# A two-convolution kernel: a later filter and even portions, loads in long rows, and two operations moved from VectorE to ScalarE

## The reference

```
x = x + wavelet_conv(groupnorm(x), w0, w1, w2, bias)
x = x + local_filter(groupnorm(x), spatial_weight)
```

```
dot        = einsum('bchw,bckhw->bkhw', x, patches)
sim        = dot / max(norm_x * norm_p, 1e-8)
weight     = (sim + 1) / 2 * spatial_weight[k]
out        = einsum('bckhw,bkhw->bchw', patches, weight)
```

## Time and profile before

| | |
|---|---|
| median of 3 runs | 2198.71 us |
| the profiled execution's own time | 2198.1 us |
| its span, first to last instruction | 2196.5 us |
| TensorE busy, matmuls | 76% of the span |
| VectorE busy | 69% |
| ScalarE busy | 29% |
| mean granted TensorE clock | 0.825 of full |
| HBM traffic | 238.7 MB read, 86.6 MB written |

### The profile page before, as it was taken

One profiled execution on the slowest core, in us unless ns is written; L12 is line 12 of the kernel. 1 busy time (PEld: TensorE's weight loads), 2 busy tenths in 40 slices (PEclk: granted clock), 3 DMA queues, 4 the chain that ended last, 5 costly groups with the idle time before them and its releaser, 6 DMA issues.

```text
span 2196.5 us, 49122 instructions
## 1 busy us (share of the span) xinstructions
PE 1666.1 (76%) x16895; PEld 883.3 (40%) x16895; DVE 1506.4 (69%) x2313; ACT 629.4 (29%) x1030; POOL 448.3 (20%) x791
## 2 busy tenths in 40 slices
PE   4777796787877797778877786778878787775575
PEld 3543353334433353334433353334433343332343
DVE  6427767876588567876588667885678666785564
ACT  2321232223332232323333232323223132322331
POOL 1352331014200232013300242012400242011000
PEclk8978997879878897788878897788978898777555
DMA  5252366564955567663956466564955567563775
GB/s 167 77 126 77 113 166 164 153 157 115 223 139 152 149 168 162 154 169 108 222 135 154 129 171 169 138 179 114 222 131 159 137 159 180 126 177 103 167 170 126
DMA packets 216642, 329.95 MB, mean 150 GB/s; under 512 B 51189, under 2 KB 182261, under 8 KB 215797
## 3 DMA queue, kind: packets, MB, share of 16 engines
q1 hardware_dynamic: 174832, 207.19, 38.4%
q0 software_dynamic: 41472, 118.24, 19.7%
HBM read 238.70 MB, written 86.61 MB: 148 GB/s over the span
## 4 chain that ended last, share of the span: by engine, by line
DVE 29%; PE 25%; issue 17%; SPq 13%; DMA 12%; DVEq 2%; ACT 2%; POOL 0%; POOLq 0%; ACTq 0%
PE conv L1258 7%; DMA unit_mem<-d_n 6%; DMA d_n<-st_n 5%; SPq L390 5%; DVE wgt L980 4%; PE conv L1232 4%; PE gram L1320 4%; SPq L398 4%; PE out_ps L1342 2%; PE vals_ps L1303 2%; DVE eo L795 2%; PE conv L1217 2%; DVE st_n L928 2%; DVE st_a L926 2%; PE conv L1441 2%
## 5 line engine op out<-in xcount | busy, mean ns | idle before, releaser
L1258 PE MATMUL conv<-thl,wconv 128*128 128x496 f16 (+2 forms) x1920 | 574.6, 431 | 20.8 <-DVE xa L855 8.3
L980 DVE SCALAR_TENSOR_TENSOR wgt<-gram,tapw 124x512 f32<-124x512 f32 x512 | 347.9, 688 | 349.2 <-PE gram L1320 316.5
L454 POOL DMA_DIRECT2D ring<-in_x x576 | 333.7, 584 | 322.3 <-ACT xa L538 222.4
L1320 PE MATMUL gram<-unit_mem 128*60 128x128 f16 x4096 | 267.6, 259 | 119.6 <-DVE wgt L980 114.7
L1342 PE MATMUL out_ps<-wgt,vals 124*32 124x128 f32 x4096 | 199.8, 323 | 122.5 <-DVE wgt L980 98.1
L1320 PEld LDWEIGHTS gram<-unit_mem 128*60 128x60 f16 x4096 | 164.3, 121 | 315.1 <-issue 309.0
L1258 PEld LDWEIGHTS conv<-thl,wconv 128*128 128x128 f16 x1920 | 174.2, 107 | 254.1 <-issue 120.5
L1232 PE MATMUL conv<-thl,wconv 128*128 128x480 f16 (+7 forms) x1200 | 251.7, 367 | 0.0
L538 ACT ACTIVATE vals<-vals_ps 124x512 f32<-124x512 f32 x128 | 76.2, 595 | 419.5 <-PE vals_ps L1303 419.5
L1342 PEld LDWEIGHTS out_ps<-wgt,vals 124*32 124x32 f32 x4096 | 115.2, 124 | 188.3 <-DVE wgt L980 124.1
L488 POOL DMA_DIRECT2D up<-d_z x128 | 68.6, 539 | 596.9 <-DVE xa L909 566.5
(11 more groups left out here) (132 smaller groups left out, 2007.2 us busy)
## 6 DMA issues: line engine op xcount, KB each, us to landing
unit_mem<-d_hl SPq DMA_DIRECT2D x512, 180.0 KB
ring<-in_x POOLq DMA_DIRECT2D x288, 128.0 KB, 3.4
ring<-in_x POOLq DMA_DIRECT2D x288, 127.0 KB, 3.5
d_hl<-st_hl SPq DMA_DIRECT2D x64, 360.0 KB
d_v<-st_v SPq DMA_DIRECT2D x64, 360.0 KB
unit_mem<-d_v SPq DMA_DIRECT2D x128, 180.0 KB
up<-d_z POOLq DMA_DIRECT2D x160, 128.0 KB, 2.8
d_x<-x POOLq DMA_DIRECT2D x32, 512.0 KB, 4.2
```

The costliest lines, as they stand in the source:

```text
L454: pool.dma_start(dst, src).then_inc(raw_in[slot], 16)
L980: V.scalar_tensor_tensor(out=dst, in0=g, scalar=SIM_SCALE ** 2, in1=tapw[:, :].unsqueeze(1).to_broadcast([KN, 2, 2 * QN]), op0=ALU.add, op ...
L1258: last = mm(dst[:, :, b0:b1], wconv0[:, w, 2 * (p % ROWS4) + s, dx + 2, :], thl[:, p % 2, d, s, :, b0 + dx:b1 + dx] if p % ROWS4 != 1 else ...
L1320: last = mm(bank[row:row + KQ, col:col + QN], key[:, q, e_at, TH * KW * g:TH * KW * g + KQ], tile[:, :, TH * g + 1:TH * g + 1 + TH, 1:1 + ...
```

## The change

It has four parts.

1. **TensorE's order.** The last `filter_group` of a unit moves into the next unit (portion 1); `key_values` of the unit moves from before its first gram product to behind its second, and its second half from portion 4 to 5. The first three `filter_group` move from portions 3, 5, 7 to 4, 5, 7. The `norm_piece` of unit `j + 2` move from portions 1, 2 to 0, 2. PE's wait for the unit's load stands where it stood, before the first gram product. SyncE's wait before loading over the buffer of unit `u - 2` is now for its gram products and turned values, not for its last `filter_group`.
2. **VectorE's portions.** The two to four instructions of `accumulate`, `finals`, `wino_in` and `image_stats`, which ran in one portion, are spread over two to four portions. `value_lows` moves from portion 2 to 0, `result` from 1 to 2, `wino_low` from 2 to 1. Four of the eight `raw_stats` of the next image go from the opening into unit 0, and the other four to the end of the opening; the first group norm's small operations go from units 0 and 1 to units 1 and 2.
3. **Long-row loads.** In DRAM a half is now laid out as [part, channel, quadrant, 720] instead of [partition, part, 720]. A load of keys, queries or values reads rows of 4 x 720 f16 (5760 B) where it read rows of 720 (1440 B), and there are 7 such loads instead of 10. The saves are 5 instead of 3; a save of a part writes from 128 partitions to a DRAM pattern whose leading dimension is the quadrant, with 4 entries.
4. **ScalarE.** The square of the root (line 920) becomes a ScalarE `Square`. The count of small norms (line 935) becomes a ScalarE `Sign` of 1.0001 - norm with a sum, and `set_flag` turns the sum of signs to a count. The second piece of `vals_out` moves behind `keep_point`.

The diff, cut to its core:

```
@@ sync: save_half, load_unit
-                sp.dma_start(d_hl[b, h], st_hl[:, :, h % 2, :]).then_inc(half_saved, 16)
-                sp.dma_start(d_v[b, h], st_v[:, :, h % 2, :]).then_inc(half_saved, 16)
+                for hl in range(2):
+                    sp.dma_start(d_hl[b, h, hl].rearrange("c q n -> q c n"), st_hl[:, hl, h % 2, :]).then_inc(half_saved, 16)
+                for hl in range(2):
+                    sp.dma_start(d_v[b, h, hl].rearrange("c q n -> q c n"), st_v[:, hl, h % 2, :]).then_inc(half_saved, 16)
...
                 if u >= 2:
-                    sp.wait_ge(group_done, START + 4 * (8 * b + u - 1))
+                    sp.wait_ge(gram_ready, 8 * (8 * b + u - 1))
+                    alone(sp)
+                    sp.wait_ge(vt_ready, 16 * b + 2 * (u - 1))
...
-                for dst, order in ((keys[s], (0, 1, 0, 1)), (queries[s], (0, 0, 1, 1))):
-                    for j, hl in enumerate(order):
-                        sp.dma_start(dst[C * j:C * j + C].rearrange("c q e n -> c q (e n)"),
-                                     d_hl[b, u, :, hl, :].rearrange("(q c) n -> c q n", c=C)).then_inc(unit_in[s], 16)
-                for hl in range(2):
-                    sp.dma_start(values[s][C * hl:C * hl + C].rearrange("c q e n -> c q (e n)"),
-                                 d_v[b, u, :, hl, :].rearrange("(q c) n -> c q n", c=C)).then_inc(unit_in[s], 16)
+                for j in range(2):
+                    sp.dma_start(keys[s][2 * C * j:2 * C * (j + 1)].rearrange("c q e n -> c (q e n)"),
+                                 d_hl[b, u].rearrange("l c q n -> (l c) (q n)")).then_inc(unit_in[s], 16)
+                for j, hl in enumerate((0, 0, 1, 1)):
+                    sp.dma_start(queries[s][C * j:C * j + C].rearrange("c q e n -> c (q e n)"),
+                                 d_hl[b, u, hl].rearrange("c q n -> c (q n)")).then_inc(unit_in[s], 16)
+                sp.dma_start(values[s][0:2 * C].rearrange("c q e n -> c (q e n)"),
+                             d_v[b, u].rearrange("l c q n -> (l c) (q n)")).then_inc(unit_in[s], 16)
@@ scalar
+                if p == 1:
+                    act.wait_ge(n2_kept, START + 16 * b + 2 * h + 2)
+                    act.wait_ge(unit_low, START + 8 * b + h)
+                    copy(st_b[:, :], st_a[:, :], func=ACT.Square).then_inc(root_squared, 1)
+            def count_own(b, h):
+                act.wait_ge(prep_link, 8 * PREP_LINKS * b + PREP_LINKS * (h + 1))
+                act.wait_ge(unit_low, START + 8 * b + h)
+                nc.scalar.activation(st_hl[:, 1, h % 2, 0:UN], st_n[:, h % 2, :], ACT.Sign, bias=edge[:, :], scale=-1.0,
+                                     accum_out=short[:, h % 2:h % 2 + 1]).then_inc(short_kept, 1)
...
                 for j in range(CONV_TILES):
-                        vals_out(b, j, 0)
...
                     if conv and j + 1 < CONV_TILES:
                         wino_high(i, j + 1)
                     if ls and j + 2 < 2 * BANDS:
-                        norms(b, j + 2)
+                        norms(b, j + 2, 0)
                     if ls:
-                        vals_out(b, j, 1)
+                        vals_out(b, j, 0)
+                    if ls and j + 2 < 2 * BANDS:
+                        norms(b, j + 2, 1)
                     if conv:
                         keep_point(i, j)
                     if ls:
+                        vals_out(b, j, 1)
                         if j + 2 < 2 * BANDS:
+                            count_own(b, j + 2)
                             unit_highs(b, j + 2)
@@ vector
-                ch.link(dve, V.tensor_tensor(st_b[:, :], st_a[:, :], st_a[:, :], ALU.mult))
+                dve.wait_ge(root_squared, 8 * b + h + 1)
...
-                prep_chain.link(dve, V.tensor_scalar(st_b[:, :], st_n[:, h % 2, :], 1.0001, None, ALU.is_lt, ALU.add,
-                                                     accum_out=short[:, h % 2:h % 2 + 1]))
...
                 if conv:
-                    for c in range(SLOTS):
-                        raw_stats(i + 1, c)
                     wino_delta(i, 0)
...
+                    raw_stats(i + 1, 0)
+                    raw_stats(i + 1, 1)
                     level1_out(i, 0)
...
                     level1_out(i, 1)
-                    raw_stats(i + 1, SLOTS + 2)
-                    raw_stats(i + 1, SLOTS + 3)
+                    raw_stats(i + 1, 2)
+                    raw_stats(i + 1, 3)
...
-                            if k == 1 and j > 0:
+                            if k == 2 and j > 0:
                                 result(b, j - 1)
-                            if k == 1 and j in (1, 3, 5, 7):
-                                accumulate(i, j - 1)
+                            if k in (1, 2) and j in (1, 3, 5, 7):
+                                accumulate(i, j - 1, k - 1)
+                            if k == 1 and j + 1 < CONV_TILES:
+                                wino_low(i, j + 1)
+                            if k < 4 and j == 0:
+                                raw_stats(i + 1, SLOTS + k)
-                            if k == 5 and j + 2 < CONV_TILES:
-                                wino_in(i, j + 2)
+                            if k in (6, 7) and j + 2 < CONV_TILES:
+                                wino_in(i, j + 2, k - 6)
@@ tensor: the hook of portion k in unit j
-                                key_values(b, j, 0)
+                                unit_here(b, j)
                             if k == 4:
-                                key_values(b, j, 1)
+                                filter_group(b, j, 0)
                             if k < PAIRS:
                                 gram(b, j, k, short_ones[0])
-                            if k in (3, 5, 7, 8):
-                                filter_group(b, j, (k - 3) // 2 if k < 8 else 3)
+                            if k == 1:
+                                if j > 0:
+                                    filter_group(b, j - 1, 3)
+                                key_values(b, j, 0)
+                            if k == 5:
+                                filter_group(b, j, 1)
+                                key_values(b, j, 1)
+                            if k == 7:
+                                filter_group(b, j, 2)
```

More of the change, by code:

```diff
@@ L639, in vals_out @@
                 act.wait_ge(vt_ready, 16 * b + 2 * u + part + 1)
-                act.wait_ge(group_done, START + 4 * (8 * b + u))
+                act.wait_ge(group_done, START + 4 * (8 * b + u) - (2 if u > 0 and part == 0 else 0))
                 copy(vals[:, 16 * part:16 * part + 16, :].rearrange("p n c -> p (n c)"), vals_ps[0:KN, :]).then_inc(vals_done, 1)
@@ L676, in iteration @@
                 for j in range(CONV_TILES):
-                    if ls:
-                        vals_out(b, j, 0)
-                    if conv and j == 1:
+                    if conv and j == 2:
                         root(gn1, gn1_var, gn1_root, i + 1)
@@ new lines, in wino_in @@
+                if step != 1:
+                    dve.wait_ge(t_ready, 8 * i + p)
+                    if kind == 0:
+                        wino_chain.link(dve, V.tensor_tensor(e2, two_rows(delta, 3), two_rows(delta, 1), ALU.subtract))
+                        wino_chain.link(dve, stt(e2, two_rows(xa, H0 // 2 * half + 3), -2.25, e2))
+                    elif kind == 1:
+                        wino_chain.link(dve, V.tensor_tensor(t2, two_rows(delta, 4), two_rows(delta, 0), ALU.add))
+                    elif kind == 2:
+                        wino_chain.link(dve, stt(e2, two_rows(delta, 3), 4.0, two_rows(delta, 1), op1=ALU.subtract))
+                    else:
+                        wino_chain.link(dve, stt(e2, two_rows(delta, 1), -4.0, two_rows(delta, 3)))
@@ new lines, in wino_in @@
+                if step != 0:
+                    if kind == 0:
+                        V.tensor_tensor(point[0], even, odd, ALU.add)
+                        V.tensor_tensor(point[1], even, odd, ALU.subtract).then_inc(t_wide, 1)
+                    elif kind == 1:
+                        stt(t2, two_rows(delta, 2), -4.25, t2).then_inc(t_wide, 1)
+                    else:
+                        far = 2.0 if kind == 2 else 0.5
+                        stt(point[0], odd, far, even)
+                        stt(point[1], odd, -far, even).then_inc(t_wide, 1)
@@ L878, in accumulate, with finals @@
                     dve.wait_ge(live_kept, n + 1)
[L879 to L886 removed]
+                acc = two_rows(xa, 2 + H0 // 2 * half + 2 * pair)
+                if kind == 0:
+                    stt(acc, acc, x_gain, s2).then_inc(acc_step, 1)
+                else:
+                    stt(acc, s2, 1.0 if pair == 0 else 4.0, acc).then_inc(acc_step, 1)
+            def finals(n, half, pair):
                 dve.wait_ge(acc_step, acc_count(n, 4 * half, SUMS_AT[3]))
@@ L1013, in iteration @@
                     sums(b, 7)
-                    finals(b, 1)
```

(5 more changed lines are left out.)

135 lines of the change are left out of this document (58 added, 77 removed).

## The result

The changed kernel takes 2318.35 us (median of 4 runs, 2315.27 to 2328.09) against 2197.97 of the kernel before beside it: 1.055 times, 95% interval 1.052 to 1.059. It is 5.5% slower where I had forecast 2067 us and a gain of 6%. The profiled execution took 2328.09 us for a span of 2326.5.

What follows compares the result with a forecast made beforehand. It took an exchange between VectorE and TensorE, read per stage, as the bound. From 2198.1 us, -144 for seven iterations and +13 for iteration 8 gave 2067, chance 0.52, own range 2030 to 2105; 8 in 10: 1978 to 2165.

Steps and rivals of the forecast that it cites:

- The bound of before, parts 1 and 2: Units 1 to 5: VectorE and TensorE wait on each other; VectorE's idle time falls from 4.2 to 1.5 us per unit.
- Part 4: Units 1 to 5: VectorE loses 1.64 us per unit, 8.2 us in all; ScalarE's added 1.4 us per unit is hidden.
- Rival C: Norms-to-split chain: table loads or late values copy make a unit some 23 us, about 2124 us; 0.20 with milder rival B.
- Part 3, the saves: Four large saves run on four DMA engines, 7.8 us in place of 2.0; loads begin after 10.1 us, not 4.2.
- the collision: Unit 0: four later raw rows collide with unit 1's load; unit 0 taken as 23.0 us, between 21 and 27.
- Both are under 20.8, but only just.: SyncE's 19.6 us and the save-and-load round trip's 20.1 per unit stay under VectorE's 20.8 us.
- SyncE's cycle: Per unit: save 10.1, load 7.0, store and residual every two units; 19.6 us with gaps, against 15 before.
- rival B: Save packets take 96 ns, a save 12.3 us; every unit waits for SyncE's cycle of 24.1 us; 2247 us, chance 0.13.
- The signs: Loads begin 10 us after first save if right, 6 Rival A, 14 rival B; units 1 to 5 over 115: core wrong.
- The sum: -18.2 + 1.4 - 2.2 - 1.6 = -20.6 us per iteration, -144 for seven; iteration 8 +13; 2067 us.
- The long rows: Loads: rows of 5760 B can't be slower per byte; seven issues replace ten, 7.0 us in place of 8.4.
- Rival A: Saves get 16 engines, SyncE's cycle is 15 us, VectorE alone binds, 104 us for units 1 to 5; 1972 us, chance 0.15.

## Why the prediction was wrong

**The bound of before, parts 1 and 2: right.** The pause at the change of unit is gone, and where no load is late VectorE is idle 1.9 and 2.2 us per unit (units 1 and 4 of the change, mean of seven), 1.5 forecast.

**Part 4: right.** VectorE's work in units 1 to 5 is 96.7 us, as forecast. ScalarE's square takes 713 ns (0.715 taken), the sign 804 plus 187 to read its sum (0.7 taken, 0.3 too little, which shows in no stretch). Rival C is refuted: still two table loads, and the variant with the new ScalarE work is the faster one.

```profile
L548 ACT ACTIVATE st_b<-st_a 128x612 f32<-128x612 f32 x64 | 45.6, 713 | 2.0
L548 ACT ACT_TABLE_LOAD x2 | 2.6, 1283 | 15.1 <-PE conv L1479 11.8 <-DVE gn L792 3.3
L651 ACT ACTIVATE st_hl<-st_n,edge 128x612 f16<-128x612 f32 x64 | 51.5, 804 | 61.0 <-DVE st_n L957 60.7
L651 ACT ACTIVATION_READ_ACCUMULATOR st_hl<-st_n,edge 128x1 f32 x64 | 12.0, 187 | 0.0
```

**Part 3, the saves: this step failed, by its size.** Four engines was right. "128 packets of 61 ns, 7.8 us in place of 2.0, so the loads begin after 10.1 us" was not. Three things were missing.

- The pace alone is 66 ns, which is 0.6 us over 128 packets, and the loads begin after 11.1 to 13.0 us even in the quiet units.
- I took that quiet time for all eight saves of an iteration. Three of them run beside raw rows and upsampled data and take 14.8 to 22.3 us. The forecast named the collision, "four raw rows now come later and collide with this load", and gave unit 0 23.0 us; it took 34.2. Beside q0 the save gets 1.4 engines of its four, and when q0 is through it still has only four, while twelve stand idle. The row for the crowd was there: 98% busy in the earlier trace rows.
- A load's landing took 4.7 us in quiet, against 2.9 taken from the earlier trace rows. The 13.7 beside raw rows is no part of the miss, since the kernel before had it too and unit 0 was forecast as a difference from it.

**The comparison that decided: "Both are under 20.8, but only just."** SyncE's cycle was put at 19.6 us. In iteration 8 it is 22.3 over a pair of units: 19.6 (2176.50 to 2196.07) in a unit without store and residual, 25.0 in one with them. The forecast's terms make 17.1 of the first (10.1 + 7.0). It lacks 1.7 us of save (2176.50 to 2188.30 is 11.8), 0.5 of load (2188.30 to 2195.83 is 7.5) and the gap; store and residual add 5.4 where 4.0 were taken. With that the bound passes from VectorE to SyncE, as rival B had it. B's mechanism and side are right; its cause, 96 ns per packet everywhere, is not (66 in quiet), and its 2247 us are too low. The signs say the same: the loads begin after 11.1 to 13.0 us in quiet units, between the forecast's 10 and B's 14, and units 1 to 5 take over the 115 us that were named as the sign of an error in the core.

**The sum.** Forecast and measured per iteration (mean of seven): unit 0 23.0 and 34.2, units 1 to 5 107.0 and 120.9, unit 6 19.8 and 22.6, unit 7 with the opening 79.5 and 86.5 (264.2 less the others): 34.9 us, 244 over seven. Iteration 8 to the end takes 213.2 us (2326.5 - 2113.32) where 185.9 + 13 were forecast, 14.3 more. 2067 + 244 + 14 = 2325, of 2328. A third of the miss is unit 0, another two fifths are units 1 to 5. That I added 13 us to the last iteration and took 144 off the others shows the weak point: where VectorE doesn't bind, I saw SyncE's loss, and where it binds by a margin of 0.7 us (20.8 against 20.1) I let the margin stand without a spread on it.

**The long rows.** "Can't be slower per byte" held, and they are some 9% faster. The forecast's 96 ns for a short row divides the time by all 1364 packets, 149 of them under 512 B; without these it is at most 108 ns. A load's eleven issues take 7.5 us where 7.0 were forecast, and the longer landing takes back what they save. Rival A, 16 engines, 1972 us, came out at 2054 with the long rows kept; its 104 us for units 1 to 5 are 108.75 there (iteration 4), and its iteration 8 wasn't reached either.

Open: the slower packets with three saves of four rows (81 ns), and the gain of 1.2% from late raw statistics beside early saves.

## What to carry to other kernels

Before a layout change for longer rows, look at the leading dimension of both sides of every DMA, the saves above all: if one is 4, split the DMA so that each leads with 32 or more, even at the price of more issues. Check for it in the trace by the DMA share between a transfer's issue and its landing: a steady quarter is four engines. And where two bounds of a pipeline lie within a few per cent, take the duration of the serial one from its crowded stretches as well as from the quiet ones.

## What I had not expected of the hardware

- The save before unit 1's load, on four engines beside other traffic, takes 18.8 to 22.3 us against 11.4 in quiet; the same bytes on 16 engines (the variant with the old DMAs) take 7.7 to 8.6 there against 4.2.
- The issue of a save on four engines can stall: 6.4 us beside other traffic for two DMAs that take 1.56 us otherwise, and 4.52 us for one in the variant with an unused row (2281.50), with a quarter of the engines busy. In the kernel before no issue of a save took over 1.1 us in iterations 1 to 7, though all engines were full before unit 1.
- Rows of 5760 B are read some 9% faster per byte (68 ns per 1000 B) than rows of 1440 B (75).
- Packets of 1440 B to DRAM take 61 ns on 16 engines, 66 on four, and 81 on four in the variant with an unused row between the quadrants.
